# Two-part float32r projections, with the first attention group's maxima among the last tiles of stage A

## The chip, the cores and the metric

The kernel runs on one core of one Trainium2 chip. TensorE (PE, with its weight loads PEld), VectorE (DVE), ScalarE (ACT), GpSimd (POOL) and SyncE (SP, which issues most DMAs) each run their own program in order and meet at semaphores. The metric is the device time of one execution in microseconds (us), the median of several runs; lower is better. Traces come from one profiled execution.

## The reference

One transformer layer on x of [4, 1024, 256], float32, 16 heads of 16 columns, 16 experts. Cut to what matters:

```python
xn = layernorm(x)
q, k, v = split(xn @ W_qkv + b_qkv)            # q and k then get rotary position factors
attn = softmax(q @ k.T / 4) @ v                # per batch and head, 1024 x 1024
a = attn @ W_out + b_out
scores = sigmoid(xn @ w_gate.T)                # 16 experts in 4 groups: the best 2 groups,
idx, w = top 4 of the experts allowed, weights divided by their sum
routed = sum over the 4 chosen of w * (silu(xn @ w1_e.T) * (xn @ w3_e.T)) @ w2_e.T
shared = (silu(xn @ w1_s.T) * (xn @ w3_s.T)) @ w2_s.T
out = x + a + routed + shared
```

## The kernel before

The work is four blocks, one after the other; a block ends when all engines have ended it.

Stage A makes everything that depends on single tokens, in 32 tiles of 128 tokens (8 tiles to a batch entry b). The tile loop is software-pipelined: in step n, ACT normalises tile n (`normalise`), PE transposes tile n-2 (`turn`), ACT copies the transpose to SBUF, PE multiplies tile n-3 with the weights `wsb` (`project`: a bias product, then float32 products of 512 columns for q and k and of 272 columns for v and the gate), ACT takes the results out, POOL multiplies q and k with the rotary factors in four operations (`sines`), and PE transposes tile n-6 back (`back`). ACT writes the first, rounded part of it to `stg` (`part1`, L432), DVE the remainder (`rest`, L366). q and k go to HBM in these two parts and serve attention as float32r operands. Results of POOL's predecessor have two buffers (`qks`), so ACT may write tile k only when POOL has finished tile k-2. For each b, DVE chooses the allowed expert groups and the limits of the best four (`route`, 30 instructions in five pieces) during five of the next eight steps; for b = 3 this comes after the last tile. DVE's program also holds the layer norm statistics of tiles 8 to 31, four tiles to each of steps 0 to 5. Because all of DVE's instructions run in the order written, whatever stands behind them waits.

Stage B is attention in 16 groups of 4 heads, each group in 16 quads (QUADS, index k); two quads' halves of queries make a group: k below 8 is the first half, above it the second. A softmax needs the row maxima of the scores first: PE makes a product `pm` of 128 queries with 1024 keys (two products of 512 columns, `max_half`, L1098), DVE reduces it (`maximum`, L1048), POOL splits the 16 maxima of a half group in two parts (`split`), DVE turns them (`turn_rows`), and SP stores them to HBM and loads them back as two more rows of the queries (`rows`), so that the score products `pst` (L1109) come out less the maximum. ACT takes the exponential (L1022), PE multiplies with the values (`pv`, L1121). The maxima run 24 ahead of the scores (AHEAD): a prologue makes 24 of group 0, with two `pm` buffers in PSUM, and each quad then makes two more. Group 0's first loads (`first_loads`) go out at the end of stage A. POOL plans the expert lists beside attention: `choose`, which needs the routing of all four b, `number_choices`, then a count of choices (two PE products with `sel`, at the end of the prologue, taken out by ACT), totals, offsets, places, and the scatter of rows (`send`).

Stage C runs 144 tiles of expert rows, stage D the shared experts, the output product and the sum.

The arrangement of all this is written by hand: the lags of the steps, and in which quad a piece of the plan stands.

## Time and profile before

| | us |
|---|---|
| Median of 3 runs (lowest, highest) | 1217.91 (1217.72, 1218.17) |
| Span of the profiled execution | 1217.1 |
| PE busy | 1150.2 (95%) |
| DVE busy | 959.9 (79%) |
| ACT busy | 750.6 (62%) |
| POOL busy | 578.9 (48%) |

Rough places in the span: stage A to 159, stage B's prologue to 198, attention to about 870, then the experts, and stage D from about 1105. An engine's busy share is a mean over all of these. A row of the timeline gives start, duration, engine, line, operation and count, and in brackets how long the engine stood idle before it and what ended that. A row of grouped instructions gives busy time and mean duration; one of the busy time by stretch gives length, busy time of each engine, the granted clock of TensorE (1.00 is 2.4 GHz, 0.50 is 1.2 GHz) and the DMA share.

### The profile page before, as it was taken

What the parts mean: (1) busy time and instruction counts of PE and PEld (TensorE: products, weight loads), DVE (VectorE), ACT (ScalarE), POOL (GpSimd) and SP (SyncE); (2) the same over time, 40 slices, a digit from 0 to 9 for tenths busy, and PEclk for the clock granted to TensorE, in tenths of its full rate; (3) what the DMA queues carried; (4) which work ended last, traced back from release to release, by engine and by line L of the source; (5) the groups of instructions that cost most, each with busy time, mean ns of one, the idle gap of its engine ahead of it and who ended that gap; (6) DMA issues with size and microseconds to landing.
All of it is one profiled execution on the core that took longest, in us unless ns stands there. A gap on an engine that the chain in (4) does not pass through costs nothing. (4 is left out here: it accounts for less than half of the span.)

```text
span 1217.1 us, 27786 instructions
## 1 busy us (share of the span) xinstructions
PE 1150.2 (95%) x8310; PEld 582.5 (48%) x8311; DVE 959.9 (79%) x1451; ACT 750.6 (62%) x1568; POOL 578.9 (48%) x861
## 2 busy tenths in 40 slices
PE   4999767999999999999999999998999999998998
PEld 2555422333333333333333333333788887875665
DVE  6575685999999999999999999970555555556888
ACT  3666303888888888888888888887333333330000
POOL 6999947354465653232322323231576666661000
PEclk9999955999999999999999999999999999999999
DMA  6466743454435453343324332402777666655765
GB/s 221 156 202 216 224 110 140 180 163 125 126 106 145 125 143 86 87 109 96 94 80 117 89 95 79 103 29 64 215 225 228 205 204 213 194 165 185 234 220 173
DMA packets 127288, 181.74 MB, mean 149 GB/s; under 512 B 41441, under 2 KB 88929, under 8 KB 125282
## 3 DMA queue, kind: packets, MB, share of 16 engines
q1 hardware_dynamic: 111842, 138.55, 39.6%
q0 software_dynamic: 15360, 42.04, 10.0%
q8 instruction: 55, 0.90, 0.3%
q14 instruction: 31, 0.25, 0.1%
HBM read 99.71 MB, written 80.81 MB: 148 GB/s over the span
## 5 line engine op out<-in xcount | busy, mean ns | idle before, releaser
L1048 DVE TENSOR_REDUCE mx<-pm 128x1 f32<-128x1024 f32 x512 | 620.6, 1222 | 31.4 <-PE pm L1098 30.6
L1022 ACT ACTIVATE pr<-pst 128x512 f32<-128x512 f32 x1024 | 556.6, 596 | 86.3 <-PE pst L1109 34.9
L1098 PE MATMUL pm<-kt,qt 48*128 48x512 f32 x1024 | 386.6, 461 | 13.4 <-DMA qt<-s_q 8.0
L1109 PE MATMUL pst<-qt,kt 50*128 50x512 f32 x1024 | 377.7, 449 | 6.5 <-DMA qt<-s_m 6.5
L1121 PE MATMUL po<-pr,vt 128*17 128x256 f32 x4096 | 322.9, 388 | 9.9 <-ACT osb L1032 9.6
L1098 PEld LDWEIGHTS pm<-kt,qt 48*128 48x128 f32 x1024 | 157.1, 192 | 237.5 <-DVE mx L1048 173.1
L1274 POOL DMA_INDIRECT s_y<-ys_c,slot_c x144 | 139.6, 969 | 85.7 <-issue 46.4
L1121 PEld LDWEIGHTS po<-pr,vt 128*17 128x17 f32 x4096 | 69.0, 95 | 198.9 <-issue 110.3
L1109 PEld LDWEIGHTS pst<-qt,kt 50*128 50x128 f32 x1024 | 152.8, 186 | 18.8 <-ACT pr L1022 10.9
L950 POOL DMA_INDIRECT s_xg<-p_rows,p_slot x128 | 125.2, 978 | 56.0 <-issue 29.8
L1354 PE MATMUL pd<-w13s,xt_c 128*128 x576 | 149.5, 382 | 0.4 <-ACT xt_c L1284 0.4
L1308 DVE TENSOR_TENSOR hb_c<-pd,sg_c 128x128 f32<-128x128 f32 x144 | 42.0, 292 | 121.0 <-ACT sg_c L1290 102.2
L1290 ACT ACTIVATE sg_c<-pd 128x128 f32<-128x128 f32 x144 | 40.0, 278 | 155.1 <-PE pd L1354 155.1
L928 POOL CAST mp<-mx 128x16 fp32r<-128x16 f32 x32 | 6.4, 199 | 264.1 <-DVE mx L1048 264.1
L1354 PEld LDWEIGHTS pd<-w13s,xt_c 128*128 128x128 f32 x576 | 99.1, 192 | 18.7 <-issue 0.6
L1367 PE MATMUL c_pY<-w2s,ht_c 128*128 x288 | 89.5, 393 | 4.1 <-DVE ht_c L1303 3.4
L1298 DVE COPY ys_c<-c_pY 128x256 f32<-128x256 f32 x144 | 60.7, 422 | 19.4 <-PE c_pY L1367 15.1
L1443 ACT ACTIVATE sg_d<-pd 128x512 f32<-128x512 f32 x16 | 9.6, 599 | 95.4 <-PE pd L1386 86.5
L457 PE MATMUL pQ<-wsb,xt_a 128*128 128x512 f32 x128 | 66.2, 641 | 0.0
L1473 DVE SCALAR_TENSOR_TENSOR spare<-yg,wk,spare 128x256 f32<-128x256 f32 x128 | 62.1, 485 | 4.6
L366 DVE TENSOR_TENSOR stg<-pR,stg 128x512 fp32r<-128x512 f32 x32 | 22.0, 691 | 47.6 <-ACT stg L432 45.9
L1284 ACT ACTIVATE xt_c<-pd 128x256 f32<-128x256 f32 x144 | 55.1, 383 | 5.6 <-PE pd L1347 4.7
(188 smaller groups left out, 1169.5 us busy)
## 6 DMA issues: line engine op xcount, KB each, us to landing
xg<-s_xg SPq DMA_DIRECT2D x144, 128.5 KB
yg<-s_y SPq DMA_DIRECT2D x32, 512.0 KB, 3.9
s_q<-stg SPq DMA_DIRECT2D x32, 256.0 KB
s_k<-stg SPq DMA_DIRECT2D x32, 256.0 KB
kt<-s_k SPq DMA_DIRECT2D x32, 256.0 KB
qt<-s_q SPq DMA_DIRECT2D x64, 128.0 KB
s_o<-osb SPq DMA_DIRECT2D x32, 256.0 KB, 6.9
w13s<-w SPq DMA_DIRECT2D x1, 4608.0 KB, 14.6
```

The lines of the kernel that those rows point to most:

```text
L457: mm = pe.matmul(pQ[t % 2][:, :], xt[:, t, c, :], wsb[:, c, 0:2 * C], start=False, stop=(c == CC - 1))
L950: pool.indirect_dma_start(out=s_xg, out_offset=bass.IndirectOffsetOnAxis(ap=plan["slot"][:, sl, k:k + 1], axis=0), in_=plan["rows"][:, sl, ...
L1022: nc.scalar.activation(pr[:, (k % 2) * 4 + ORDER[i], :], pst[bank(gg, k, i)][:, :], ACT.Exp, scale=SCALE).then_inc(exp_ok, 1)
L1048: nc.vector.tensor_reduce(mx[:, half, col:col + 1], pm[slot][:, :, :].rearrange("p a n -> p (a n)"), AX.X, ALU.max).then_inc(mx_free, 1)
L1098: mm = pe.matmul(pm[slot][:, kk, :], qt[buf][rows, half, pair, qi * P:(qi + 1) * P], kt[buf][rows, pair, kk * 512:(kk + 1) * 512], start=T ...
L1109: pe.matmul(pst[bank(buf, k, i)][:, :], kt[buf][rows, pair, kc * P:(kc + 1) * P], qt[buf][rows, half, pair, :], start=True, stop=True)\
L1121: mm = pe.matmul(po[32 * h:32 * h + VW, cols], vt[buf][:, k % 8, h * VW:(h + 1) * VW], pr[:, (k % 2) * 4 + h, cols], start=(k % 8 == 0 and ...
L1274: pool.indirect_dma_start(out=s_y, out_offset=bass.IndirectOffsetOnAxis(ap=slot[:, t:t + 1], axis=0), in_=ys[:, t, :], in_offset=None).the ...
L1298: nc.vector.tensor_copy(ys[:, t, :], pY[t % 2][:, 0:C]).then_inc(ys_ok, 1)
L1354: mm = pe.matmul(pG[t % 2][:, 0:2 * F], xt[:, t % 2, c, :], w13[:, c, chosen(t), :].rearrange("p a n -> p (a n)"), start=(c == 0), stop=(c ...
L1367: pe.matmul(pY[t % 2][:, 0:C], ht[:, t % 2, :], w2[:, chosen(t), :].rearrange("p a n -> p (a n)"), start=True, stop=True).then_inc(yy_ok, 1)
L1473: ins = v.scalar_tensor_tensor(out=acc[:, k % 4, :], in0=yg[:, k % BUF_Y, n, :], scalar=keep["wk"][:, k, n:n + 1], in1=acc[:, k % 4, :], o ...
```

## The change

Stage A. The weights are split once into `wh` (rounded to float32r, by ACT) and `wl` (the remainder, by POOL). Each transposed tile is copied twice by ACT, to `xt` and, rounded, to `xh`; DVE subtracts the two (`low`, giving `xl`). A float32 product becomes three float32r products: `xh wh`, `xh wl`, `xl wh`. `project` now waits for `xl_ok`. The transposes and the v product have one PSUM buffer instead of two; one of the freed pairs becomes `pm0`.

All 32 maxima of attention's group 0 are made in stage A, two in each of steps 22 to 37, in that one buffer: the second waits for the reduction of the first. Group 0's keys and queries are loaded at step 15. The split, turn, store and load of the first half's maxima stand at steps 31 and 32. The routing of b = 3 moves from the end of stage A to the start of stage B. PE ends stage A with FILL = 4 float32 products whose results are not used.

Stage B. There is no prologue. Quads 0 to 3 of group 0 have no maxima. `choose` comes after the routing, `number_choices` and the planning pieces some quads later than before; the count products stand in quad COUNT = 13 of group 0, in `pm0`, with ACT's two copies at the same place. The stores of the last tiles, the load of the expert weights and the value load of group 1 come later in SP's program. The sent tiles shift accordingly (two at a time up to j = 3). Stage D's first addition waits for its product by a semaphore of its own (`bv_ok`), and its `sg` shares memory with the routing's buffers. The rest is the same.

```diff
+        wh, wl = sb("wh", [P, CC, W], F32R), sb("wl", [P, CC, W], F32R)
+        xh, xl = sb("xh", [P, 2, CC, P], F32R), sb("xl", [P, 2, CC, P], F32R)
...
-        pT = [ps(f"pT{i}", [P, 512]) for i in range(2)]
+        pT = ps("pT", [P, 512])
         pQ = [ps(f"pQ{i}", [P, 512]) for i in range(2)]
-        pV = [ps(f"pV{i}", [P, 512]) for i in range(2)]
+        pV = ps("pV", [P, 512])
...
+                if buf == 0:
+                    pool.wait_ge(const_ok, 7)
+                    pool.wait_ge(w_in, 17)
+                    nc.gpsimd.tensor_tensor(wl[:], wsb[:], wh[:].bitcast(F32), ALU.subtract).then_inc(w_in, 1)
+                    pool.wait_ge(w_in, 18)
...
+                if n == SPLIT_A:
+                    pool.wait_ge(mx_free, 16)
+                    split_maxima(nc, own, first, 0, mp_ok)
...
+            def low(k, t, b):
+                dve.wait_ge(xt_ok, k + 1)
+                v.tensor_tensor(xl[:, t % 2, :, :], xt[:, t, :, :], xh[:, t % 2, :, :].bitcast(F32), ALU.subtract)\
+                    .then_inc(xl_ok, 1)
...
+            for n in range(NT + BACK):
+                t, b = n % TPB, n // TPB
+                if n < NT:
+                    other_stats(n, t, b)
+                if 0 <= n - PROJ < NT:
+                    low(n - PROJ, (n - PROJ) % TPB, (n - PROJ) // TPB)
+                early(n, 0)
+                if n >= BACK:
+                    rest(n - BACK, (n - BACK) % TPB, (n - BACK) // TPB)
+                early(n, 1)
+                early(n, 2)
+                if TPB <= n < NT:
+                    routing(n - TPB, t, b - 1)
+                if n == TURN_A:
+                    turn_rows(nc, dve, first, 0, 0, 0)
...
             def project(k, t, b):
-                pe.wait_ge(xt_ok, k + 1)
+                pe.wait_ge(xl_ok, k + 1)
                 need(pe, qks_ok, k - 1)
                 pe.matmul(pQ[t % 2][:, :], ones3[:], bias3[:, 0:2 * C], start=True, stop=False)
                 for c in range(CC):
-                    mm = pe.matmul(pQ[t % 2][:, :], xt[:, t, c, :], wsb[:, c, 0:2 * C],
-                                   start=False, stop=(c == CC - 1))
+                    for n, (a, w) in enumerate(splits):
+                        mm = pe.matmul(pQ[t % 2][:, :], a[:, t % 2, c, :], w[:, c, 0:2 * C],
+                                       start=False, stop=(c == CC - 1 and n == 2))
...
+            for n in range(NT + BACK):
+                if n >= BACK:
+                    back(n - BACK, (n - BACK) % TPB, (n - BACK) // TPB)
+                early(n, 0)
+                if 0 <= n - TURN < NT:
+                    turn(n - TURN, (n - TURN) % TPB, (n - TURN) // TPB)
+                k = n - PROJ
+                if 0 <= k < NT:
+                    project(k, k % TPB, k // TPB)
+                early(n, 1)
+                if 0 <= k < NT:
+                    project_v(k, k % TPB, k // TPB)
+                early(n, 2)
+            pe.wait_ge(qks_ok, NT)
+            for _ in range(FILL):
+                pe.matmul(pQ[0][:, :], xt[:, TPB - 1, 0, :], wsb[:, 0, 0:2 * C], start=True, stop=True)
...
+FIRST_LOADS = 15
+FILL = 4
+EARLY = {n: 2 for n in range(22, 38)}
+SPLIT_A, TURN_A, ROWS_A = 31, 31, 31
...
+            for piece in range(5):
+                route(nc, dve, routed, first["gb"], keep, B - 1, piece, first["ex_ok"], first["ex_used"], keep["passed_dve"])
+            dve.sem_inc(route_ok, 1)
...
+                        if counting:
+                            counts(place(g, k, 0) - 1)
...
+                        if counting:
+                            pe.wait_ge(keep_ok, 2)
+                            for m in range(2):
+                                for kk in range(2):
+                                    max_half(pe, first, mbuf, us[m], m, place(g, k, m), kk, place(g, k, m) - 1)
```

## Rows read from the trace of the kernel before

**Rows 1.** The page's head: span of the profiled execution.
```profile
span 1217.1 us, 27786 instructions
```

**Rows 2.** Busy time by stretch: length, PE, PEld, DVE, ACT, POOL, clock, DMA.
```profile
26.00:122.00 96.00, 94.95 (x366) 54.11 (x366) 56.81 (x100) 61.20 (x155) 92.27 (x96) 1.00 0.58 187
```

**Rows 3.** POOL's groups from 16 to 147 us, and its last tile's start.
```profile
L287 POOL TENSOR_TENSOR rc<-qks,ropesb 128x512 f32<-128x512 f32 x31 | 39.7, 1280 | 0.0
L283 POOL TENSOR_TENSOR rs<-qks,ropesb 128x256 f32<-128x256 f32 x31 | 22.8, 735 | 10.0 <-ACT qks L413 10.0
...
147.21 0.72 POOL L283 TENSOR_TENSOR rs<-qks,ropesb 128x256 f32<-128x256 f32 x1
```

**Rows 4.** Timeline, one tile on PE: start, duration, engine, operation, idle before.
```profile
60.18 0.39 PE L455 MATMUL pQ<-bias,ones 3*128 3x512 bf16 x1
60.49 1.98 PE L457 MATMUL pQ<-wsb,xt_a 128*128 128x512 f32 x4
61.03 0.19 PEld L457 LDWEIGHTS pQ<-wsb,xt_a 128*128 128x128 f32 x1 [0.24 <-issue]
...
63.98 0.39 PE L455 MATMUL pQ<-bias,ones 3*128 3x512 bf16 x1
```

**Rows 5.** Timeline, the joint: first maximum, first scores and their partners.
```profile
160.07 1.22 PE L1098 MATMUL pm<-kt,qt 48*128 48x512 f32 x4 [8.05 <-DMA qt<-s_q]
161.32 2.36 DVE L1048 TENSOR_REDUCE mx<-pm 128x1 f32<-128x1024 f32 x2 [2.61 <-PE pm L1098]
...
198.41 0.79 PE L1109 MATMUL pst<-qt,kt 50*128 50x512 f32 x1 [6.30 <-DMA qt<-s_m]
...
199.00 0.63 PE L1109 MATMUL pst<-qt,kt 50*128 50x512 f32 x2
...
199.43 1.05 PE L1098 MATMUL pm<-kt,qt 48*128 48x512 f32 x2
```

**Rows 6.** Busy time by stretch: the prologue's maxima, and the first four quads.
```profile
163.00:190.00 27.00, 25.18 (x46) 10.56 (x45) 24.41 (x23) 1.08 (x2) 15.84 (x15) 0.50 0.48 126
198.40:213.30 14.90, 14.89 (x81) 5.47 (x81) 9.40 (x8) 8.59 (x16) 7.55 (x16) 0.50 0.40 140
```

**Rows 7.** The page's costliest groups: the maxima on DVE, the exponentials on ACT.
```profile
L1048 DVE TENSOR_REDUCE mx<-pm 128x1 f32<-128x1024 f32 x512 | 620.6, 1222 | 31.4 <-PE pm L1098 30.6
L1022 ACT ACTIVATE pr<-pst 128x512 f32<-128x512 f32 x1024 | 556.6, 596 | 86.3 <-PE pst L1109 34.9
```

**Rows 8.** Timeline, the start: DVE's statistics, PE's first tile, POOL's first operation.
```profile
16.04 7.93 DVE L349 BATCH_NORM_STATS2 bnst<-xs 128x6 f32<-128x256 f32 x24
...
18.14 0.34 PEld L457 LDWEIGHTS pQ<-wsb,xt_a 128*128 128x128 f32 x1 [0.52 <-issue]
...
21.72 0.72 POOL L283 TENSOR_TENSOR rs<-qks,ropesb 128x256 f32<-128x256 f32 x1 [9.99 <-ACT qks L413]
```

**Rows 9.** DVE's routing beside POOL and alone (stretches), and two of its groups.
```profile
115.20:138.10 22.90, 20.81 (x76) 11.67 (x75) 18.82 (x35) 10.91 (x30) 22.11 (x24) 0.93 0.63 200
148.80:158.75 9.95, 0.74 (x4) 0.42 (x4) 9.03 (x33) 0.60 (x1) 2.29 (x2) 0.65 0.73 200
...
L366 DVE TENSOR_TENSOR stg<-pR,stg 128x512 fp32r<-128x512 f32 x6 | 4.1, 691 | 4.6 <-ACT stg L432 3.9 <-DVE spare L546 0.4
...
L500 DVE TENSOR_TENSOR g_ge<-g_ge,g_lt 128x128 f32<-128x128 f32 x1 | 1.4, 1368 | 0.0
```

**Rows 10.** Timeline, POOL: start of choosing, start and end of numbering.
```profile
159.20 0.32 POOL L562 MEMSET p_ca<- 128x256 f32 x1 [7.98 <-POOLq L141]
...
182.14 1.04 POOL L553 TENSOR_TENSOR p_ca<-spare 128x512 f32<-128x512 f32 x1
...
205.18 0.24 POOL L582 TENSOR_SCALAR p_ws<-p_rank 128x32 f32<-128x32 f32 x1 [0.20 <-POOL p_rank L630]
```

**Rows 11.** Busy time by stretch: a pause of PE, and the half clock after it.
```profile
128.00:130.00 2.00, 0.04 (x1) 0.00 (x0) 0.29 (x1) 0.92 (x3) 1.87 (x3) 1.00 0.97 317
131.50:134.70 3.20, 3.20 (x7) 1.73 (x6) 2.88 (x12) 1.13 (x3) 3.07 (x4) 0.51 0.58 152
```

More of the change, by code:

```diff
@@ L98, in rounds, with rounds_last @@
         emit(j)
-def rounds_last(eng, n, emit):
-    emit(0)
-    with eng.Fori(1, n - 1) as j:
+def rounds_last(eng, n, emit, head):
+    for j in range(head):
+        emit(j)
+    with eng.Fori(head, n - 1) as j:
         emit(j)
@@ L340, in _ @@
             setup = own.n
+            first["setup"] = setup
             def other_stats(k, t, b):
[L344 removed]
+                if b:
                     return
@@ L375, in routing, with early @@
                 assert t != TPB - 1 or own.n == ROUTE_LINKS, own.n
-            steps(dve, B, TPB, NT, [(0, other_stats), (BACK, rest), (TPB, routing)])
+            def early(n, spot):
+                use = early_use(n, spot)
+                if use is not None:
+                    row_maximum(nc, dve, first, use, 0, use)
+            for n in range(NT + BACK):
[13 more added lines that the diff above has]
+                    turn_rows(nc, dve, first, 0, 0, 0)
         @block.scalar
@@ L1003, in body @@
                             send(*tile)
-            for j in range(3):
+            for j in range(4):
                 body(j)
-            with pool.Fori(3, NG // 2 - 1) as j:
+            with pool.Fori(4, NG // 2 - 1) as j:
                 body(j)
```

380 lines of the change are left out of this document (213 added, 167 removed).

## The prediction

> **What bounds the kernel now.** I read the page's totals first, then the busy time by stretch, then each engine's rows inside the first 215 us, since nearly every edit lies there; the profiled span is 1217.1 us [rows 1]. The reader is to see four things. (1) In the tile loop of stage A, POOL is busy 92.27 of 96 us [rows 2] with four operations per tile, two of each kind shown, 2 x 0.735 + 2 x 1.28 = 4.03 us [rows 3]. Tile 0 starts on POOL at 21.72 [rows 8] and tile 31 at 147.21 [rows 3], so a tile costs (147.21 - 21.72) / 31 = 4.05 us. PE's own work for a tile is 3.8 us (bias to bias, 60.18 to 63.98) [rows 4]. (2) Between the last tile and attention lies a joint: the b = 3 routing on DVE until 158.7, a first maximum product at 160.07 that waited for a DMA, its 23 followers, and the first score at 198.41, again behind a DMA [rows 5]. (3) There the granted clock is at half, 1.2 GHz; the four quads 198.4 to 213.3 took 14.9 us [rows 6]. (4) After that, attention is DVE's: 512 maxima at 1.222 us, 31.4 us of idle in all [rows 7]. So the joint, 147.2 to 213.3, is what can be won; from the fifth quad of group 0 (213.3) on both kernels do the same work.
>
> **Stage A starts later.** The weight splits add an ACT copy and a POOL subtraction of 1568 columns; at 0.6 [rows 7] and 1.28 us [rows 3] per 512 columns that is about 1.8 and 3.9 us. That takes 5.7 us from the landing of the weights; unless they land after 21.3 - 5.7 = 15.6, `low`, below, covers it: I take nothing, and 5.7 if that cover goes. The new `low` costs more. A projection now waits for it, and DVE's program puts it behind the statistics of steps 0 to 3: 16 instructions at 0.33 us from 16.04, till 21.3. Project 0 starts at 21.9. PE is slow there (loads of weights for the 512-column passes come every 0.34 + 0.52 = 0.86 us in that stretch [rows 8], every 0.19 + 0.24 = 0.43 later [rows 4]), so bias plus six products take about 3.0 us; with the ACT copy, 0.6, and handovers POOL starts at 25.9, 4.2 later than 21.72 [rows 8]. Between nothing (if POOL caught up, which 96% busy excludes) and 5.3 I take 4.2.
>
> **Projections.** No row has a float32r product over 128 rows. Bounds: a float32r product of 512 columns over 48 rows took 0.43 us at the half clock (starts of scores and their partners at 199.00 and 199.43) [rows 5], so 0.21 at full; the float32 ones take 0.43 per pass, four passes a tile. Six at 0.21 to 0.43 are 1.3 to 2.6 us against 1.72. Six of 272 columns are by columns 0.7 to 1.4 against 0.9. I take 1.3 and 0.9, since both float32r rows at hand run one pass at the column rate: PE saves 0.4 us a tile, worth nothing while POOL bounds. ACT gains one copy of 256 columns, under 0.6 us; it is busy 61.20 of 96 us [rows 2], so it stays under POOL.
>
> **Steps 3 to 21 stay POOL's.** Project 19 (step 22) starts near 25.9 + 18 x 4.05 = 98.8. PE, at 3.8 a tile or less, leads POOL by most of a tile, since `qks` has two buffers, but routing steps put `low` 0.5 + subtraction 0.69 [rows 9] + routing 16.06 / 5 = 3.2 on DVE, 4.4 to 4.7 us, and eat the lead. I take 99.8, between 96 and 102.
>
> **Steps 22 to 34, two maxima each, one slot.** This decides. Start a step where `low` ends. Project takes 1.62 (the bias 0.31, 60.18 to 60.49 [rows 4], and 1.3), the second product and its way to DVE 0.73 (two passes of 0.21 and 0.3 of latency; at half clock 160.07 to 161.32 was 1.25 [rows 5]), its reduction 1.22, two handovers 0.1: 3.67 us. Without routing, the next project waits only for the next first product and the turn (0.85): 4.42 us, over POOL's 4.05. With routing DVE goes on first with routing and `low`, and these lie under POOL's own work. The same 30 instructions took 18.82 - 4 x 0.69 = 16.06 us beside POOL and 9.03 - 2 x 0.69 = 7.65 alone [rows 9]; the reduction never stretched (1.222 mean, 512 of them). I take 16.1. Seven gaps hold routing (after steps 22, 23, 27 to 31): one whole batch and pieces 3 and 4 of another (some 6.6), 22.7 in all. Seven times 3.67 + 0.5 is 29.2, so 51.9; five others make 22.1; `turn_rows` waits for POOL's split about 0.8. The first reduction pair ends at 99.8 + 1.62 + 0.73 + 1.22 = 103.4, the last at 178.2. `low` has no row: a subtraction of 256 columns should take about half of the 0.69 that 512 cost, 0.35; small DVE operations took up to 1.4 us beside POOL (1368 ns for a 128-column one [rows 9]); over seven gaps that is -1 to +6 us against my 0.5.
>
> The rows show DVE's reduction from PSUM unmoved and its small SBUF operations stretched. The Trainium skill, GPSIMD Engine Reference, section 1 (Specifications), says that GpSimd's SBUF interface is shared with VectorE, with contention for DVE instructions with two SBUF inputs; `low` is one. By it every `low` would be of the stretched kind and the sum 6 us longer.
>
> **Tail, joint and first quads.** Steps 35 to 37 hold six maxima in one slot: 0.73 + 1.22 + 0.1 = 2.05 each, 12.3 us, till 190.5. FILL is four float32 products of two passes, 4 x 0.86 = 3.4 us on PE, of which DVE's last reduction covers 1.5: 1.9 more. A block change costs 0.5 (DVE ends at 158.7 [rows 9], POOL starts at 159.20 [rows 10]). First score at 192.9; it waits for no DMA, since the rows went out at step 31. The four quads without maxima are ACT's: 16 x 0.59 [rows 7] is 9.4 us, and DVE's last routing alone, 7.65 plus gaps, fits under them. Fifth quad: 202.4 against 213.3, a gain of 10.9.
>
> **Given back later.** At quad 13 of group 0 PE does the counts, the quad's scores and values, waits for two ACT copies and only then the maxima: DVE idles about 1.8 us (counts 0.43, a quad at full clock half of 14.9 / 4, 1.9, a product 0.43 and 0.3 of latency, less one reduction, 1.22). Choosing now starts after routing and numbering after it; numbering takes 23.3 us (182.14 to 205.42) [rows 10] and the next split 0.3 before DVE turns it; DVE comes there 8 quads of (620.6 + 31.4) / 256 = 2.55 and two maxima later, 22.8 us: 0.8 us late. Moved stores, weights, value loads and plan pieces go past queues with slack; nothing. Sum: 1217.1 - 10.9 + 2.6 = 1208.8 at a full clock.
>
> **The clock.** PE idles about 3 us in each of the seven routing gaps (3.8 - 0.4 + 4 x 0.21 = 4.2 us of work in 7.3). Before, a pause of 2 us (128 to 130, PE busy 0.04 us) was followed by half clock from about 131.5 to 134.7, with PE dense [rows 11]; and maxima alone, PE busy 25.18 of 27 us, did not bring it back [rows 6]. One such stretch costs at most 2.05 us on the chain (project and second product doubled), often less, since values and transposes are off the chain. Zero to 14 us; I take 3 for the seven gaps and 2 for the tail and a slow start of FILL: 1213.8. The median of the runs is 0.8 above the profiled span, so **1214.6**.
>
> The trace shows no stretch of transposes alone, so the next sentence stands on the page only. The Trainium skill, TensorE: Matmul & The Clock Gate, Part 4 (PE-mode transpose), says that transposes don't count as PE activity the same way; by it the back and turn steps don't help to hold the clock and the third rival below gains weight.
>
> **Rivals.** *The cover is better:* with POOL starved in the routing steps, DVE's operations fall between their two prices, (16.1 + 7.65) / 2 = 11.9 a batch: 22.7 becomes 16.8, 5.9 saved, and no half clock, another 5: 1203.7. For it: POOL has 4.03 us of work in a 7.3 us step. Against: it falls just on the routing. *A mere shift:* `low` always stretched (+6), project at 0.3 us a product (+0.5 x 12): 1214.6 + 6 plus some of the rest, about 1220, the same within 0.2%. *Slower:* each of the seven gaps lets the clock fall over the whole chain (14.4), and the tail and FILL run at half (6 x 0.43 + 3.4 = 6.0): 1208.8 + 20.4 = 1229.2, and 0.8: 1230. It decides from the point where a gap in PE's work exceeds about 2 us; for it speak the rows of 128 to 135, against it that there the clock came back after 3.2 us of dense work and that a stretch often misses the chain.
>
> **Chances.** Forecast 0.45 (own range 1208 to 1220; two thirds of it faster), better cover 0.22, mere shift 0.13, slower 0.20. The 8-in-10 range takes the better cover's centre and half of the slow one: 1203 to 1229. A measurement of this kernel can tell about 0.2%, 2.4 us, so "same" is 1215.5 to 1220.3. Faster: 0.22 + 0.30 + 0.01 = 0.53. Same: 0.12 + 0.09 = 0.21. Slower: 0.03 + 0.03 + 0.20 = 0.26.
>
> **What the profile after would show.** POOL's first `rs` at 25.9, its spacing 4.05 until the early maxima and 4.4 or some 7.3 us among them; DVE over 90% busy from about 100 to 178; two maxima at 2.05 us each in the tail; the first score near 193 and full clock there; four quads in 9.4 us; one DVE gap of 1.8 us at quad 13. Wrong it would be if routing costs DVE 12 a batch or less, if the half clock covers the early steps, or if PE and DVE don't alternate in the one slot as costed.

## The result and the profile after

The changed kernel takes 1262.66 us (median of 4 runs, 1252.74 to 1270.37) against 1217.82 of the kernel before beside it (4 runs, 1216.75 to 1218.17): a ratio of 1.038 [1.033, 1.043]. It is slower by about 45 us, where 3 us less was forecast, and it spreads over 18 us where the kernel before spreads over 1.4. The profiled execution is its fastest: a span of 1251.1, 34.0 over the 1217.1 of [rows 1]. The ratios of this document leave out executions that a lower granted clock made slower than the others of their kernel; the traces come one from each run, and that of before_fill_2 is of such an execution.

From the page of the changed kernel: busy times, the granted clock in 40 slices of the span (31 us each), and the two groups that answer to [rows 7].

```profile
span 1251.1 us, 27680 instructions
PE 1163.7 (93%) x8446; PEld 612.4 (49%) x8447; DVE 977.2 (78%) x1484; ACT 758.9 (61%) x1599; POOL 585.8 (47%) x862
PEclk9988867899899999999999999999999999999999
L602 DVE TENSOR_REDUCE mx<-pm 128x1 f32<-128x1024 f32 x512 | 620.9, 1222 | 55.9 <-PE pm L592 55.2
L1156 ACT ACTIVATE pr<-pst 128x512 f32<-128x512 f32 x1024 | 556.3, 597 | 90.3 <-PE pst L1211 38.8
```

The work itself is unchanged: the same 512 maxima at 1222 ns, the same exponentials at 597. What grew is DVE's idle time ahead of the maxima (31.4 to 55.9) and the low clock, which in the kernel before fills two slices (the sixth and seventh) and here spreads over the third to the eighth.

Where the 34.0 went, by marks of the two traces:

| mark | before | after | moved by |
|---|---|---|---|
| tile 0 projected (step 3) | 16.6 | 23.7 | +7.1 |
| tile 19 projected (step 22) | 91.2 | 111.9 | +20.7 |
| tile 31 projected | 142.9 | 205.5 | +62.6 |
| first score | 198.4 | 228.4 | +30.0 |
| second turning of rows (quad 4 of group 0) | 216.4 | 240.9 | +24.5 |
| last turning of rows | 815.8 | 849.6 | +33.8 |
| end of the span | 1217.1 | 1251.1 | +34.0 |

(In a second trace of the kernel before, below, tile 31 is projected at 140.5 and the first score comes at 197.0.) A turning of rows is DVE's `turn_rows`; from one to the next is a half group. The attention from quad 4 on costs 9.3 us, the first score 30.0, and quads 0 to 3 give 5.5 back.

Stage A by stretch, in the changed kernel and in the second trace of the kernel before. Columns: length, busy time of PE, PEld, DVE, ACT and POOL, granted clock, DMA share, GB/s.

```profile
26.00:122.00 96.00, 76.83 (x375) 59.30 (x374) 60.89 (x128) 52.41 (x142) 80.31 (x80) 0.89 0.52 158
165.00:186.00 21.00, 19.72 (x52) 11.58 (x51) 12.99 (x27) 6.01 (x15) 8.35 (x9) 0.51 0.42 139
```

```profile
26.00:122.00 96.00, 94.95 (x366) 54.09 (x366) 57.42 (x100) 60.83 (x155) 92.26 (x96) 1.00 0.58 188
```

This is [rows 2] again, and the main finding in two lines: before, POOL is busy 92 of 96 us and PE 95, at full clock. After, PE is busy for 77 us at a mean clock of 0.89, and POOL, which was to stay the bound, for 80. It waits for qks, ACT for pQ, and PE for xl. The waits of the changed kernel from 16 to 228 us (engine, tile and line, what it waited for: us in total, times, longest):

```profile
ACT qks L462 <- PE pQ L507: 71.6, 30, 6.9
POOL rs L297 <- ACT qks L462: 60.0, 19, 10.0
PE pQ L504 <- DVE xl L385: 30.3, 15, 4.1
DVE stg L391 <- ACT stg L481: 29.1, 11, 4.4
```

The kernel before, second trace, 16 to 197 us:

```profile
DVE stg L366 <- ACT stg L432: 45.6, 16, 8.0
```

In the kernel before, DVE waits 45.6 us in `rest` for ACT and nobody is the worse for it: nothing that PE needs soon comes out of DVE. In the changed kernel `low` stands behind that same wait. One such step, first DVE, then PE (start, duration, idle time before and what ended it):

```profile
59.33 0.69 DVE L391 TENSOR_TENSOR stg<-pR,stg 128x512 fp32r<-128x512 f32 x1 [3.60 <-ACT stg L481]
59.94 1.04 DVE L653 TENSOR_SCALAR work<-work 128x128 f32<-128x128 f32 x1
61.01 0.95 DVE L654 RECIPROCAL work<-work 128x128 f32<-128x128 f32 x1
62.00 1.05 DVE L646 TENSOR_TENSOR work<-work 128x64 f32<-128x64 f32 x2
63.08 0.84 DVE L385 TENSOR_TENSOR xl<-xt_a,xh 128x256 fp32r<-128x256 f32 x1
```

```profile
59.98 0.41 PE L498 MATMUL pT<-ident,xn_a 128*128 128x128 f32 x2
63.98 0.60 PE L504 MATMUL pQ<-bias,ones 3*128 3x512 bf16 x1 [3.58 <-DVE xl L385]
64.51 0.80 PE L507 MATMUL pQ<-wh,xh 128*128 128x512 f32 x1
```

`rest` ended 3.60 late, a routing piece of 3.0 followed, then `low`, and PE stood 3.58. The first product behind the bias took 0.80 us, where at full clock it takes 0.50 (at 137.78): the granted clock fell to half at 62.8, inside the pause.

### The profile page after: what moved, and what is told of

Read it like the earlier page. It is cut to its first block and busy times, and to the rows that moved or that the text cites. A ratio compares the mean times of both kernels' runs of the same rounds, so it can differ in the third digit from the quotient of the medians.

```text
span 1251.1 us, 27680 instructions
## 1 busy us (share of the span) xinstructions
PE 1163.7 (93%) x8446; PEld 612.4 (49%) x8447; DVE 977.2 (78%) x1484; ACT 758.9 (61%) x1599; POOL 585.8 (47%) x862
## 5 line engine op out<-in xcount | busy, mean ns | idle before, releaser
L602 DVE TENSOR_REDUCE mx<-pm 128x1 f32<-128x1024 f32 x512 | 620.9, 1222 | 55.9 <-PE pm L592 55.2
L592 PE MATMUL pm<-kt,qt 48*128 48x512 f32 x1024 | 382.3, 454 | 11.7 <-DVE mx L602 11.7
L1211 PEld LDWEIGHTS pst<-qt,kt 50*128 50x128 f32 x1024 | 152.0, 185 | 19.5 <-ACT pr L1156 15.1
L1461 PEld LDWEIGHTS pd<-w13s,xt_c 128*128 128x128 f32 x576 | 99.2, 192 | 18.6 <-issue 0.6
L1551 ACT ACTIVATE work<-pd 128x512 f32<-128x512 f32 x16 | 9.6, 597 | 95.4 <-PE pd L1494 86.5
L462 ACT ACTIVATE qks<-pQ 128x512 f32<-128x512 f32 x32 | 19.2, 599 | 71.6 <-PE pQ L507 71.6
L1454 PE MATMUL pd<-ident,xg 128*128 128x128 f32 x288 | 56.0, 277 | 2.5 <-PEq L918 2.5
```

The costliest lines, as they stand in the source:

```text
L592: mm = pe.matmul(first["pm"][slot][:, kk, :], first["qt"][buf][rows, half, pair, qi * P:(qi + 1) * P], first["kt"][buf][rows, pair, kk * 5 ...
L602: nc.vector.tensor_reduce(first["mx"][:, half, col:col + 1], first["pm"][slot][:, :, :].rearrange("p a n -> p (a n)"), AX.X, ALU.max).then ...
L1211: pe.matmul(pst[bank(buf, k, i)][:, :], kt[buf][rows, pair, kc * P:(kc + 1) * P], qt[buf][rows, half, pair, :], start=True, stop=True)\
L1454: mm = pe.transpose(pT[t % 2][:, c * P:(c + 1) * P], xg[:, t, c * P:(c + 1) * P], ident[:])
L1461: mm = pe.matmul(pG[t % 2][:, 0:2 * F], xt[:, t % 2, c, :], w13[:, c, chosen(t), :].rearrange("p a n -> p (a n)"), start=(c == 0), stop=(c ...
```

## The experiments

There were eighteen further runs, in five sets, each beside the kernel before. In sets 1, 4 and 5 every kernel was granted less clock (the kernel before takes 1381 to 1399 there, at a mean granted clock of 0.87 to 0.90, against 1214 to 1217 at 0.97 in sets 2 and 3), mostly from about 280 us on. Why is not known: the record gives chip 0 for set 1 and for set 3 alike, so it can't be put down to the chip. Stage A is the same: variants of the kernel before have their first score at 196.8 to 198.3 there, 197.0 here. So from sets 1, 4 and 5 the marks up to the first score are read, and their ratios only with care.

### The two parts of the change, each alone

`plain` takes the projections back and keeps the early maxima; `split_only` puts the split projections into the kernel before.

```
 plain:       project: pe.wait_ge(xt_ok, k + 1)   # was xl_ok
              pe.matmul(pQ, xt[:, t, c, :], wsb[:, c, ...])   # one product for three
              (no low, xh, wh, wl)
 split_only:  before.py + wh, wl, xh, xl, three products each,
              steps(dve, ..., [(0, other_stats), (PROJ, low), (BACK, rest), (TPB, routing)])
```

> The changed kernel with the projections back to single float32 products from xt and wsb (no xh, xl, wh, wl: no second ACT copy, no DVE low, no POOL subtraction of the weights), the early maxima, FILL and the rest of the change kept. Theory A (the DVE subtraction `low`, which stands in DVE's order behind rest, the root links and the routing, holds PE up in nearly every step with routing, and each pause is followed by a stretch at half clock): the steps up to 21 return to POOL's spacing of 4.05 us, tile 19 is projected near 98 to 100 instead of 111.9, the first score comes at 200 to 208 instead of 228.4, and the kernel takes 1221 to 1232. Theory B (the maxima on the one pm, 2.05 us of DVE and PE each, cost it whatever the projections are): tile 19 gains, but the first score stays past 220 and the kernel past 1243.

> The kernel before with the two-part float32r projections alone (wh and wl, xh, xl, three products each, project waiting for low), two pT and two pV as before, its 24 maxima after the last tile, its planning unchanged. Theory A: POOL's first rs is near 28 (before 21.72), the steps with routing are spaced 6 to 8 us instead of 4.05 as in the changed kernel, so that stage A ends 10 to 20 us later: 1228 to 1240. Theory B: only the later start shows, the rest stays POOL-bound at 4.05: 1220 to 1225. If the routing pauses cost nothing because POOL covers them: 1216 to 1220.

Both were repeated later, as `plain_2` (set 3) and `split_only_2` (set 4), and both kernels of the case as `before_again` and `after_again` (set 2):

> The changed kernel with single float32 projections, once more, on such a chip: first score 198 to 204, fifth quad some 9.5 later, attention 8 to 9 longer than in the kernel before: 1216 + 3 - 5.5 + 9 = 1220 to 1230, ratio 1.000 to 1.012.

> The kernel before with the two-part float32r projections alone, on such a chip. Theory A (the split carries the loss): first score 218 to 226, attention as in the kernel before (599 to 602 between the second and the last turned rows), ratio 1.016 to 1.024. If the first run's 223 came of its chip's clock: 203 to 210, ratio 1.004 to 1.010.

> The kernel before, unchanged, to have its stage A and its attention traced on the same chip as the runs beside it. By all theories: first score at 198 to 200 if stage A is at full clock as before, later by some us if the chip grants less; no difference to the kernel before beside it (ratio 1.00 within its interval).

> The changed kernel, unchanged, on the same chip. By all theories: first score 225 to 232, 24 to 34 us behind before_again, ratio 1.03 to 1.04 to the kernel before.

| run | tile 0 | tile 19 | tile 31 | first score | half clock, 16 to 200 us | ratio |
|---|---|---|---|---|---|---|
| before_again | 16.6 | 91.2 | 140.5 | 197.0 | 52.1 | 0.999 [0.997, 1.001] |
| plain | 17.4 | 92.5 | 176.5 | 199.5 | 30.6 | 1.013 [1.001, 1.024] |
| plain_2 | 17.5 | 92.5 | 175.0 | 197.9 | 23.8 | 1.018 [1.013, 1.024] |
| split_only | 23.3 | 115.5 | 175.6 | 223.3 | 62.5 | 1.038 [1.028, 1.047] |
| split_only_2 | 23.3 | 116.1 | 170.6 | 218.6 | 64.2 | 1.016 [1.009, 1.023] |
| after (the profile) | 23.7 | 111.9 | 205.5 | 228.4 | 65.5 | 1.038 [1.033, 1.043] |
| after_again | 23.7 | 111.6 | 204.4 | 228.5 | 71.6 | 1.038 [1.033, 1.044] |

The four corners, by first score: neither part 197.0 to 198.4, the maxima alone 197.9 to 199.5, the split alone 218.6 to 223.3, both 228.4. Up to the first score the split carries 20 to 30 us. The early maxima, with some 5 us of FILL that goes with them, carry next to nothing there: what they save behind the last tile (tile 31 to first score falls from 56.5 to 23.0) they cost in front of it (tile 19 to 31 rises from 49.3 to 82.5). Theory B, that they are the loss, falls for stage A.

For the time of the whole it is not the split alone: without it the changed kernel still stands at 1.018, with it at 1.038, so of some 46 us 22 are in the rest of the change, and they lie in the attention (below). PSUM's single buffers for the transposes and v are in plain too and delay nothing there up to tile 19 (92.5 against 91.2). That split_only reaches tile 19 four us later than the changed kernel, with nothing early in it, stays unexplained.

For split_only theory A held in the marks: POOL's first rs at 27.6, tile 31 at 171 to 176, both late as expected. Of its two ratios, 1.016 lies inside the 1.009 to 1.018 that 1228 to 1240 come to and 1.038 above; the expected attention of 599 to 602 can't be read at that clock. plain gained more than theory A said (tile 19 at 92.5, not 98 to 100; first score 199.5, not 200 to 208), and plain_2 met its first score (197.9 for 198 to 204) but not its ratio (1.018 for 1.000 to 1.012): its attention takes 619.0 us between the second and the last turning of rows, not 608. before_again (197.0 for 198 to 200) and after_again came out as expected, the one a us early.

### What the split waits for

`low_early` moves one call, and was run twice:

```
 for n in range(NT + BACK):          # DVE
     other_stats(n)
-    low(n - PROJ)
     early(n, 0)
     rest(n - BACK)
+    low(n - 2)                      # TURN is 2, PROJ 3: same tile one step sooner, ahead of routing
     early(n, 1); early(n, 2); routing(n - TPB)
```

> The changed kernel with one line of DVE's order moved: low for tile n-2 right after rest of step n, ahead of the step's routing, instead of low for tile n-3 at the head of the next step, behind the routing. Same operations, same buffers. Theory A: PE no longer waits for xl behind routing; the pauses of 2 to 3.5 us in steps 7 to 21 shrink to under 1 us, tile 19 is projected near 102 (111.9), first score 200 to 212 (228.4), time 1230 to 1245. Theory B (maxima): only steps up to 21 gain, the first score stays past 218 and the time is 1250 to 1258. If rest itself, not the routing, is what low waits behind: no change, 1255 to 1268.

> The changed kernel with low for tile n-2 right after rest of step n, ahead of the routing, once more, on a chip that grants the full clock in the attention. Theory A: first score 208 to 216 (212.1 in the run before this, 228.4 in the changed kernel), ratio to the kernel before 1.018 to 1.030 (the changed kernel 1.038). If the order of low does not matter: 1.033 to 1.043.

First score 212.1 and 216.5 (228.4), tile 19 at 105.2 and 104.7; ratio of the second 1.024 [1.019, 1.029], of the first, in set 1, 1.026 [1.017, 1.034]. The first scores lie 0.1 and 0.5 us past the expected ranges, and tile 19 three us past the 102 that was named. Where low stands in DVE's order is worth 12 to 16 us of the 20 to 30. PE's waits for xl from 24 to 110 us: changed kernel, low_early_2, split_only_2, in this order.

```profile
PE pQ L504 <- DVE xl L385: 18.6, 7, 4.1
```

```profile
PE pQ L504 <- DVE xl L385: 10.9, 7, 3.6
```

```profile
PE pQ L471 <- DVE xl L384: 14.6, 6, 3.8
```

They fall by 7.7 and do not go, since low still stands behind rest. In low_early_2 the step shown above reads, on DVE:

```profile
56.37 0.69 DVE L391 TENSOR_TENSOR stg<-pR,stg 128x512 fp32r<-128x512 f32 x1 [3.60 <-ACT stg L481]
56.98 0.71 DVE L385 TENSOR_TENSOR xl<-xt_a,xh 128x256 fp32r<-128x256 f32 x1
57.62 1.30 DVE L653 TENSOR_SCALAR work<-work 128x128 f32<-128x128 f32 x1
```

So theory A holds in the main, with rest's wait as a second part of it beside the routing. Another 6 us of the 20 to 30 are the later start (tile 0 at 23.7, in plain at 17.4). The remainder is not taken apart by any run; ACT's second copy and the length of low itself are in it.

That length goes with POOL's instructions. Of the 32 `low` in stage A, 22 took over 0.5 us, up to 1.53, and each of the 22 ended 0.28 or 0.29 us after the end of an instruction of POOL, as if it had stood still until that was over. The mean of all 32 is 0.77, where 0.5 was forecast.

### Is it the pause, or the half clock behind it?

`filled`, and again `filled_2`, put unused products into the pauses:

```
 def project(k, t, b):
+    need(pe, qks_ok, k - 1)            # was behind the wait for xl_ok
+    if k >= 5 and 1 <= t <= 5:
+        for _ in range(6):
+            pe.matmul(pQ[t % 2], wh[:, 0, 0:P], wh[:, 0, 0:2 * C], start=True, stop=True)
     pe.wait_ge(xl_ok, k + 1)
```

> The changed kernel with six unused products (wh by wh, 128 by 512 columns, float32r, about 0.23 us each, 1.4 in all) in PE's order right before the wait for xl, in the steps that follow a routing piece or the root links (tiles with t from 1 to 5, from tile 5 on); they go into the pQ that the projection then overwrites. Theory C (it is the half clock after each pause that costs most, and the pause itself little): the granted clock stays at full in more of stage A, first score 210 to 222, time 1245 to 1257. If the pauses themselves are the cost, or the products only lengthen a PE-bound step: 1260 to 1280.

> The changed kernel with the six unused products ahead of the wait for xl, on a chip that grants the full clock in the attention. If the half clock is the cost of stage A (65 to 72 us of the stretch 16 to 200 are at half clock in the changed kernel, 24 in the first run with the products): first score 205 to 212. If the pauses are the cost and the clock little: first score 219 to 226 with under 35 us at half clock; ratio 1.025 to 1.038.

First score 221.2 and 226.6; ratios, in sets 1 and 4, 1.031 [1.022, 1.040] and 1.013 [1.007, 1.018], which for one and the same kernel don't agree, and the second lies outside the 1.025 to 1.038 that were expected. PE's stretches, filled_2:

```profile
26.00:122.00 96.00, 86.80 (x433) 67.09 (x432) 61.28 (x127) 52.49 (x142) 80.40 (x80) 0.94 0.50 157
122.00:190.00 68.00, 60.96 (x265) 39.22 (x264) 53.16 (x78) 25.05 (x66) 39.54 (x42) 0.95 0.51 162
```

Time at half clock between 16 and 200 us falls from 65 to 72 us to 24 and 27. POOL is busy 80.4 of 96 us, as in the changed kernel, and the first score gains 2 to 7 us. The first run, at 221.2, lies inside theory C's band of 210 to 222, by 0.8; the second, at 226.6, outside it. Up to tile 19 nothing is gained (111.4 and 112.2 against 111.9 and 111.6), though half clock falls from 17 us to 7; between tiles 19 and 31 5 to 7 us are (86.9 and 88.1 against 93.6 and 92.8), for some 34 us less of it. Some 40 us of half clock, then, are worth 2 to 7 us in stage A, net of the products' own time: 1.4 us stand in each of 16 steps, and not all of it falls into pauses. The waits for xl carry the larger part, and theory C, by which half clock costs most, is not borne out; what the clock alone is worth stays open.

What the unused products at the joint do shows in `nofill_tiles` (set 3; it also moves plan_tiles, for which see below):

```
-FILL = 4
+FILL = 0
-    if isinstance(g, int) and g == 2 and k == 4:     # DVE: plan_tiles
+    if isinstance(g, int) and g == 2 and k == 2:
```

> The changed kernel with FILL 0 (no unused products before the attention) and with DVE's plan_tiles at quad 2 of group 2 instead of 4; the two act at places of their own. FILL took 5.8 to 6.5 us at half clock. If it only costs: first score 222 to 223 (228.4), quads 0 to 3 unchanged at 9.4 to 10. If it is what brings the clock back: the first quads run at half clock, so that the fifth quad's maxima start as late as before (237 to 240). plan_tiles: the third group's first half group 19.9 to 20.8 us instead of 22.4; if something else holds the rows (the memset of 1.8 us, the send of rows), 22 or more.

FILL in the changed kernel:

```profile
222.33 5.82 PE L553 MATMUL pQ<-wsb,xt_a 128*128 128x512 f32 x8
228.45 0.70 PE L1211 MATMUL pst<-qt,kt 50*128 50x512 f32 x3 [0.30 <-PEq L142]
```

Without it the first score comes at 225.3, 3.2 sooner, but the clock stays at half to 248.2, and first score to second turning of rows takes 19.3 us. With FILL the clock is back at full before the first score in all eleven traces that have it. In seven it stays, and that stretch takes 12.5 us; in four it falls again 2 to 4 us after the first score, and the stretch takes 17.6 to 18.9. Stretches of after_again, one of the four (first score at 228.5):

```profile
222.00:227.00 5.00, 5.00 (x7) 1.88 (x7) 1.00 (x1) 0.00 (x0) 0.00 (x0) 0.50 0.00 0
227.60:230.60 3.00, 2.25 (x7) 0.66 (x5) 1.86 (x5) 1.61 (x4) 0.66 (x2) 1.00 0.27 25
231.00:247.00 16.00, 16.00 (x83) 4.72 (x82) 6.96 (x27) 8.63 (x17) 8.45 (x10) 0.50 0.06 21
```

By the first maximum of quad 4 (237.8 in the profile of the changed kernel, 242.9 in after_again, 240.1 without FILL) the products gain 2.3 us where the clock stays and lose 2.8 where it does not. Why it stays in some traces only is open. The ratio without them, 1.052 [1.048, 1.056], is above the changed kernel's 1.038 [1.033, 1.044] in set 2 by more than these rows explain.

### Transfers that were moved past the stores

In the changed kernel SP issues the first group's loads at step 15, ahead of the stores that free stg for tile 16. ACT in the changed kernel, then in plain_2, then SP's queue in plain_2:

```profile
115.49 0.60 ACT L481 ACTIVATE stg<-pR 128x512 fp32r<-128x512 f32 x1 [5.45 <-DMA s_k<-stg]
```

```profile
103.99 0.60 ACT L471 ACTIVATE stg<-pR 128x512 fp32r<-128x512 f32 x1 [11.67 <-DMA s_k<-stg]
76.98 2.09 SPq L880 DMA_DIRECT2D kt<-s_k  x4
79.11 2.38 SPq L880 DMA_DIRECT2D qt<-s_q  x4
84.75 1.57 SPq L553 DMA_DIRECT2D s_q<-stg  x2
86.37 4.22 SPq L553 DMA_DIRECT2D s_k<-stg  x2
```

In the kernel before (second trace) those stores begin at 80.1, and ACT's wait for them is 2.2. Among the kernels with the loads ahead, the sooner stage A runs, the longer this wait: 3.3 and 5.5 in the changed kernel, 9.3 and 9.8 in low_early, 11.7 and 13.8 in plain. It takes back part of what a better stage A gains. Three kernels moved the loads behind the stores:

```
 late_loads:  FIRST_LOADS 15 -> 18; EARLY = {n: 2 if n < 34 else 3 for n in range(24, 38)};
              SPLIT_A, TURN_A, ROWS_A = 33, 33, 33
 plain_late:  the same, with the plain projections
 mix:         plain projections, FIRST_LOADS 17, EARLY {n: 3 if n in (24, 32) else 2 for n in
              range(23, 38)}, and DVE's plan_tiles at quad 2 of group 2
```

> The changed kernel with FIRST_LOADS 18 instead of 15 (the first group's keys and queries are loaded behind the stores of the second batch's stg half, not ahead of them), and so the early maxima from step 24 on: two in each of steps 24 to 33, three in 34 to 37; split, turn and rows at step 33. Theory D (the loads put ahead in SP's queue delay the store that frees stg, and ACT's part1 of tile 16 waits for it, 5.45 us in the changed kernel, 9.3 and 13.8 where stage A runs earlier): that wait falls under 2.5 us, first score 4 to 6 us earlier than after_again, ratio lower by 0.003 to 0.005. If routing and clock fill the time anyway: first score within 2 us of after_again. If the concentrated maxima of steps 34 to 37 (12 at 2.05 to 2.54, one more each) cost it: up to 5 us later.

> Both: projections from single float32 products (no low, xh, wh), and FIRST_LOADS 18 with the maxima from step 24. In the run with plain projections alone tile 19 was projected at 92.6 and then ACT waited 13.8 us for the store that frees stg; first score 199.5. Theory A plus D: that wait falls to under 4, first score 188 to 194, quads 0 to 3 shorter by 5.5, attention longer by up to 9: ratio to the kernel before 0.993 to 1.000. If the maxima on the one pm decide from step 24 on: first score 196 to 202, ratio 1.003 to 1.013.

> Single float32 projections; FIRST_LOADS 17 (the first loads right behind the stores of the second batch's half, no longer ahead of them), early maxima from step 23 (three in 24 and 32); and in the attention DVE's plan_tiles at quad 2 of group 2 instead of quad 4, so that GpSimd, which waited 9.43 us for it and then gave the maxima's rows 1.65 us late, is done before. Expected: ACT's wait for the store falls from 13.8 to 3 to 5 us, first score 192 to 199; the half group that holds that quad 19.9 to 20.8 instead of 22.4: ratio 0.993 to 1.003. If, as in the run with FIRST_LOADS 18, the first maximum waits for its loads (109) and the tail runs at half clock: first score 203 to 213, ratio 1.006 to 1.020.

None gained. late_loads: first score 236.8, 8 us later than after_again where 4 to 6 sooner was expected and 5 later at worst, ratio 1.047 [1.039, 1.056]; the wait at tile 16 was gone but came back a batch later (4.25 at 136.1), and the last twelve maxima ran on the one pm at 2.54. plain_late: 212.7, 1.027 [1.019, 1.035], past both of its ranges. mix: 203.6, 1.019 [1.015, 1.023], which is the second of its two expectations; ACT's wait fell to 3.9, and PE waited for the loads in its place:

```profile
104.98 1.22 PE L580 MATMUL pm<-kt,qt 48*128 48x512 f32 x2 [9.88 <-DMA qt<-s_q]
```

In each of these arrangements either the stores are late or the loads are. Whether the loads could go out beside the stores, from another engine's queue, was not tried.

### The attention

Between the second and the last turning of rows the kernel before takes 599.4 and 599.0. Every traced kernel with the changed planning takes more, in sets 2 and 3 and in the profile of the changed kernel: 608.7, 623.8, 612.2, 614.2, 618.6, 619.0, 618.8, 616.6 (after, after_again, late_loads, plain_late, low_early_2, plain_2, mix, nofill_tiles). All of it lies in the first ten half groups; from 455 us on they have the same 19.9 as before. The rows of the changed kernel, DVE, then PE, then POOL:

```profile
264.14 1.23 DVE L602 TENSOR_REDUCE mx<-pm 128x1 f32<-128x1024 f32 x1 [3.14 <-PE pm L592]
326.84 0.21 DVE L620 STREAM_TRANSPOSE mt<-mp 128x32 f32<-128x32 f32 x1 [1.65 <-POOL mp L611]
412.56 0.21 DVE L620 STREAM_TRANSPOSE mt<-mp 128x32 f32<-128x32 f32 x1 [1.02 <-POOL mp L611]
398.21 0.50 PE L1211 MATMUL pst<-qt,kt 50*128 50x512 f32 x1 [2.01 <-DMA qt<-s_m]
322.59 0.22 POOL L844 TENSOR_TENSOR p_d<-p_d,p_inside 128x16 f32<-128x16 f32 x1 [9.43 <-DVE p_inside L868]
```

The first is the count at quad 13. The one at 326.84: POOL's planning waits 9.43 for p_inside, which DVE now makes at quad 4 of group 2, the very quad whose rows POOL is to give; before, it was made at quad 2 of its group. In the rows at 398.21 and 412.56 the maxima's rows come late while POOL pads and sends. mix and nofill_tiles put plan_tiles at quad 2: the half group falls from 22.4 to 20.4 us in both, as expected, and the sum does not fall with it. `before_shift` makes the changed planning alone, in the kernel before:

```
-            number_choices(...)                       # POOL, ahead of group 0
+    if g == 0 and not half: number_choices(...)       # in the second half group
-    if 4 * j + i < 5: planning(4 * j + i)
+    if 2 <= 4 * j + i < 7: planning(4 * j + i - 2)
     (sends two half groups later; DVE's counts at g == 1, k == 11, tiles at g == 2, k == 4;
      weights loaded in groups 2 and 3)
```

> The kernel before with the planning in the attention moved as the change moves it and nothing else: number_choices in the second half group, the five pieces of GpSimd's planning two half groups later, the first sends of rows in the eighth, DVE's counts at quad 11 of group 1 and its tiles at quad 4 of group 2, the weights' load in groups 2 and 3; counting, maxima and stage A as before. Theory E (late rows: GpSimd waits 9 us for DVE's tiles and gives the split late, 1.65 us, later rows 1 to 2 us, and the clock falls behind each such wait): the attention takes 606 to 614 instead of 599, ratio 1.005 to 1.013. If the planning is hidden and the count products at quad 13 with the half clock of the start are the whole: 599 to 601, ratio 0.999 to 1.001.

From the second to the seventh turning it is 101.4 us in before_again and 109.3 in before_shift; the five half groups take 21.2, 22.7, 23.4, 22.5, 19.5 against 20.3, 21.1, 19.9, 20.1, 19.9. The 22.5 is the half group of plan_tiles, 2.4 more than before; the 23.4 holds 6.8 us at half clock. So the shift costs some 8 us there, and theory E holds for the place, on this one trace. Its sum of 606 to 614 can't be read: behind that stretch every kernel of set 4 was granted less clock. The ratio, 0.987 [0.980, 0.995] where 1.005 to 1.013 was expected, went the other way, and neither bears the theory out nor, in a set with such clocks, refutes it. What takes the sum from 608.7 to 623.8 between two executions of one kernel goes with half clock: 6.8 us of it inside that sum in the one and 38.0 in the other, and the half groups that grew most, from 22.8 to 29.7 and from 19.9 to 26.8, hold 17.1 and 13.7 of them.

### Half clock while PE is busy

In the kernel before, the clock is at half from 152 to 213, in its second trace from 148 to 216, and a PE that pauses seemed the reason. `before_fill` (set 4), `before_fill_2` and `before_rows` (set 5) fill PE's gaps there:

```
 scores_max(0, use, use % 2, use)
+if 4 <= use < AHEAD - 2:
+    for n in range(2):                    # before_fill: 48 rows
+        pe.matmul(pst[n], qt[0][0:KR, 0, 0, 0:P], kt[0][0:KR, 0, 0:512], start=True, stop=True)
                                           # before_rows: kt[0][:, 0, 0:P] by kt[0][:, 0, 0:512]
```

> The kernel before with two unused products (48 rows, 128 by 512 columns, float32r) behind each of the maxima 4 to 21 ahead of the attention, where PE waits for DVE and the clock is at half from 147 or 151 to 214 or 217. If the clock rises and what is left runs at full: maxima at 1.22 instead of 1.27, quads 0 to 3 in 9.4 to 11 instead of 14.9: 4 to 7 us less, ratio 0.994 to 0.997. If the clock stays at half, PE has 1.8 us for each maximum instead of 1.27: 8 to 10 us more, ratio 1.006 to 1.009.

> The kernel before with two unused 48-row products behind each of the maxima 4 to 21, once more. If what its first trace showed holds (first score at 196.8 as before, the clock back at 205 instead of 214 to 217, the second turned rows 4.5 us earlier): ratio 0.994 to 0.998. If the chip of the first run alone made it so: 0.999 to 1.002.

> The same with products over all 128 rows of kt, in the same places. If what counts for the grant is rows in use, not only PE being busy: the clock is back at full within the maxima (by 180), they are spaced 1.22 instead of 1.27, and the first quads are at full clock: ratio 0.992 to 0.996. If rows do not matter: as before_fill_2, within 0.002 of it.

Stretches of before_fill, then one of before_rows, in which every second pair of products is one of the unused:

```profile
170.00:180.00 10.00, 10.00 (x33) 7.50 (x32) 9.19 (x9) 0.00 (x0) 1.94 (x3) 0.50 0.25 75
200.00:205.00 5.00, 5.00 (x34) 1.47 (x32) 3.11 (x4) 2.84 (x6) 3.84 (x8) 0.50 0.52 184
205.00:210.00 5.00, 5.00 (x52) 1.72 (x48) 4.62 (x5) 3.94 (x9) 1.51 (x8) 0.99 0.37 141
```

```profile
170.00:200.00 30.00, 30.00 (x54) 12.98 (x52) 16.14 (x15) 0.00 (x0) 8.63 (x11) 0.50 0.32 104
```

PE was busy for 30 us without a gap, half of its products over all 128 rows, and the clock stayed at half. The expectation of before_rows failed on both sides: no return by 180, and the maxima, with four products at half clock between them, went to 2.30 each (ratio 1.007 [1.003, 1.011]). With 48 rows the products cost nothing, though the clock stayed at half beside them, which neither side of the first expectation had; the first score stayed at 196.8 and 197.6, and full clock came back at 205 and 208 instead of 213 and 216; first score to second turning took 15.2 and 16.1 us instead of 18.0 and 19.5. The ratios, 0.985 [0.975, 0.996] and 0.998 [0.994, 1.002], are from sets 4 and 5; only the first is clear of 1, on three executions, and the second, on eight, is not. So no version is shown to beat the kernel before; this is the one that may, by the 3 us of its traces. What holds the clock down from about 150 on stays open.

## Why the prediction was wrong

**The start** (POOL's first rs forecast at 25.9, measured 28.0; before 21.7 [rows 8]). The queue of low(0) behind 16 statistics was seen; not that POOL's subtraction of the weights (3.48 us at 10.79) and the memsets that it pushes behind itself would run beside DVE's root links and hold them up, two of eight columns taking 1.87 and 1.63:

```profile
10.79 3.48 POOL L285 TENSOR_TENSOR wl<-wsb,wh 128x1568 fp32r<-128x1568 f32 x1 [2.60 <-ACT wh L430]
12.43 1.87 DVE L339 TENSOR_TENSOR nwt<-rstd 128x8 f32<-128x8 f32 x1
14.34 3.65 POOL L281 MEMSET kt<- 32x2048 f32 x2
14.54 1.63 DVE L341 TENSOR_SCALAR nwt<-nwt 128x8 f32<-128x8 f32 x1
```

The same links take 0.17 before. The first ended at 14.30, the subtraction at 14.28; the second at 16.16, the first of the two memsets at 16.13. So each lasted as long as POOL's instruction beside it. The kernel before has one such case (an operation of 1.36 us at 10.40, ended at 11.76, POOL's last memset at 11.73), which the changed kernel does not; in all the next statistics begin at 18.01 instead of 16.04. The split of the weights was costed at nothing by its landing and costs 2 us by its neighbour. The Trainium skill (GPSIMD Engine Reference, section 1, Specifications) says that GpSimd's SBUF interfaces are shared with VectorE, with contention for DVE instructions with two SBUF inputs or in a 2-port perf mode. The trace agrees for the link at 12.43, which has two inputs, both `rstd`; the one at 14.54 has one, and whether it is of the second kind no run shows. The prediction had cited this for `low` and not for the links.

**Steps 3 to 21 bound by POOL at 4.05** ([rows 3]; tile 19 forecast at 99.8, measured 111.9). This step failed, and with it the rest. Its argument was busy time: PE got lighter, DVE had room [rows 2], so POOL stays the bound. But low made DVE, an engine with 45.6 us of harmless waiting and 4-us pieces of routing in a fixed order, a link between ACT and PE in each step. 2.1 of the 12.1 us are the start; from 24 to 110 us PE waited 18.6 us for xl. POOL's lead covered part of that: of the 18 gaps between its tiles, 15 are 4.0 to 4.5 us as forecast, and three, 5.7, 5.9 and 7.0, lose 6.4. The prediction saw routing put 4.4 to 4.7 us on DVE in a step and took 1.0 us for all of these steps together; DVE's wait for stg ahead of low had no term, and in the step shown above it is 3.60 us.

**Steps 22 to 34** (pairs of maxima from 103.4 to 178.2; measured 118.0 to 209.4). 14.6 us come from in front; 16.6 more are mis-sized periods. A step without routing takes 4.98 (137.46 to 142.45 to 147.43) where 4.42 was forecast, at full clock and with PE busy in all of it:

```profile
137.46:147.43 9.97, 9.97 (x47) 6.30 (x47) 7.06 (x9) 5.34 (x16) 8.20 (x9) 1.00 0.37 107
```

So PE's own work sets that step, where the prediction took PE and DVE in turn and left the v products and the transposes back out; it had PE's work at 4.2. A step with routing takes 8.8 to 9.5 from 154.6 to 190.9 where 7.3 was forecast. There the clock has a part: in filled_2, at full clock to 186, the same steps take 7.2 to 8.3, unused products included. DVE was to be busy for over 90% from 100 to 178; it is for 72%.

**The joint.** Six maxima in the tail: 12.3 forecast, 14.2 measured, 2.04 each at full clock and 2.54 at half. FILL: 3.4 us on PE forecast, 1.9 of them behind DVE's last reduction; 5.8 measured, mostly at half clock, and 4.5 of them behind that reduction (223.66 to 228.15). The prediction had 2 us for the clock in both together; it is 4.5. First score: 192.9 forecast, 228.4.

**Loads costed at nothing.** SP's loads moved ahead of the stores: ACT waited 5.45 for the store. The edit was in the diff, and the queue it passed was not walked.

**Quads 0 to 3** at the exponentials' pace, 9.4: right in the profiled execution (228.4 to 237.8), and 14.4 in the second (228.5 to 242.9), where the clock fell back to half at 230.8.

**The attention**: 2.6 forecast for count gap and numbering, measured 9.3 and 24.8. The count gap is 3.14 instead of 1.8. Missed was DVE's plan_tiles at the quad whose rows POOL owes, and what late rows then cost in clock.

**The clock** was given 5 us, 3 for the steps with routing and 2 for the joint. For the steps that is near what filled gives (2 to 7, net); for the joint it is 4.5. What the prediction did not see is that the time of one kernel varies by 18 us with it (granted clock 0.963 in the fastest execution, 0.945 in the slowest).

**The rival "Slower"** (1230, chance 0.20) had the right sign and the wrong mechanism: half clock in seven routing gaps. The range ended at 1229, 34 under the median. No rival had "low makes PE follow DVE's order in every step", though the row that prices it, DVE's waits for stg, was in the trace of before. "The cover is better" and "A mere shift" both rested on steps 3 to 21 bound by POOL.

## What to carry to other kernels

When an edit puts a new step of an engine between two others, ask what that engine is waiting for and what stands in its order ahead of the step, not how busy it is: waiting that cost nothing becomes part of the chain. A test of that kind of edit is cheap: move the step to each place in the order that its inputs allow (12 to 16 us here, for one line), and run the edit alone in the old kernel. Work moved forward into an engine's slack costs its own time if the engines wait for each other there; in plain the maxima saved 33.5 us behind the last tile and cost 33 in front of it, 12 to 14 of them in ACT's wait for a store that their loads had delayed.

## What the hardware showed that was not expected

- TensorE's granted clock stayed at half for 30 us in which PE had no gap, half of the products over all 128 rows (before_rows), and for 61 and 68 us in the two traces of the kernel before; it came back in the first quads of the attention. In after_again it fell after 3.4 us at full and stayed at half for 20.5, with PE busy 16.0 of 16.0 us from 231 to 247.
- Half clock cost little where PE waits for other engines: some 40 us less of it gained 2 to 7 us, net of the products that brought it.
- The kernel before took 1214 to 1217 us in two sets of runs and 1381 to 1399 in three, the granted clock 0.97 and 0.88; the first 200 us were alike.
- Vector instructions of eight columns took 1.87 us beside a big subtraction on POOL and 1.63 beside a memset, 0.17 without; these and 22 of the 32 `low` ended at a fixed time, 0.02 to 0.03 and 0.28 to 0.29 us, after an instruction of POOL.
